# Columns outside the related square: summed as adjacency bytes times bf16 parts, scaled at the end

## The reference, cut to what matters

```
h = max(layernorm(x), 0)
q, k = per head (8 heads of 64): h[sub] @ Wq.T + bq,  h[obj] @ Wk.T + bk      # 10000 related pairs, indices < 1500
scores[head, sub, obj] = q . k / 8;  0 on the other neighbours;  -inf where adj is 0;  1e-7 on the diagonal
attn = softmax(scores, axis=2)
x = x + (attn.sum over heads / 8) @ h
```

## Time and profile before

| | us |
|---|---|
| median of 3 runs | 1131.22 |
| lowest, highest run | 1126.92, 1132.14 |
| the profiled execution | 1126.64 |
| its span, first to last instruction | 1124.9 |
| TensorE busy, whole span | 1050.8 |
| VectorE busy, whole span | 917.9 |
| ScalarE busy, whole span | 786.5 |

### The profile page before, as it was taken

One profiled execution on the slowest core, in us unless ns is written; L12 is line 12 of the kernel. 1 busy time (PEld: TensorE's weight loads), 2 busy tenths in 40 slices (PEclk: granted clock), 3 DMA queues, 4 the chain that ended last, 5 costly groups with the idle time before them and its releaser, 6 DMA issues. The chain is left out here.

```text
span 1124.9 us, 25112 instructions
## 1 busy us (share of the span) xinstructions
PE 1050.8 (93%) x10560; PEld 715.8 (64%) x10565; DVE 917.9 (82%) x1259; ACT 786.5 (70%) x833; POOL 277.0 (25%) x272
## 2 busy tenths in 40 slices
PE   1999997999999999999988599999999999999997
PEld 1444443444444444444444499999999999999743
DVE  2355146899999999999981899999999999999466
ACT  1244336777777777776633799999999999998122
POOL 2778750000000000000000244334344344434000
PEclk9999998999999999999999799999999999999999
DMA  9640443322212221100054587767777777777311
GB/s 336 162 29 2 114 91 77 79 68 68 66 40 41 68 59 59 38 20 29 23 215 155 156 196 186 183 171 180 183 187 183 191 203 180 181 182 184 122 69 75
DMA packets 71552, 136.45 MB, mean 121 GB/s; under 512 B 9237, under 2 KB 18834, under 8 KB 69394
## 3 DMA queue, kind: packets, MB, share of 16 engines
q1 hardware_dynamic: 50386, 101.19, 25.7%
q0 software_dynamic: 21056, 33.67, 20.4%
HBM read 92.92 MB, written 25.04 MB: 105 GB/s over the span
## 5 line engine op out<-in xcount | busy, mean ns | idle before, releaser
L1511 ACT ACTIVATE area_h<-area_a,keep 128x2048 fp8e4<-128x2048 f32 x197 | 376.8, 1989 | 4.2 <-PE psum L1666 4.1
L1665 PE MATMUL psum<-s_V,area_h 128*128 128x99 bf16 x3072 | 298.1, 209 | 0.8 <-DVE area_b L1437 0.5
L1665 PEld LDWEIGHTS psum<-s_V,area_h 128*128 128x128 fp8e4 x3072 | 283.4, 98 | 1.1 <-DVE area_h L1561 0.7
L1666 PE MATMUL psum<-s_V,area_b 128*128 128x99 bf16 x2048 | 204.1, 209 | 0.0
L1666 PEld LDWEIGHTS psum<-s_V,area_b 128*128 128x128 fp8e4 x2048 | 189.5, 97 | 0.0
L743 PE MATMUL psum<-area_h,f_region 128*128 128x512 f32 x384 | 184.9, 596 | 0.0
L1185 DVE SCALAR_TENSOR_TENSOR f_region<-area_b,s_r,f_region 128x1500 f32<-128x1500 f32 x96 | 170.8, 1779 | 2.2
L1561 DVE TENSOR_TENSOR area_h<-area_h,area_a 128x512 uint32<-128x512 uint32 x256 | 167.9, 686 | 4.4
L1196 DVE CUSTOM_DVE_ANT_0 area_b<-psum,late 128x1500 f32<-128x1500 f32 x96 | 161.1, 1715 | 8.2 <-PE psum L658 8.1
L1668 PE MATMUL psum<-s_V,area_h 128*128 128x198 bf16 x1024 | 150.0, 249 | 13.7 <-DVE area_h L1561 13.7
L977 ACT ACTIVATE area_b<-area_b,s_negm 128x1500 f32<-128x1500 f32 x96 | 147.8, 1540 | 20.9 <-DVE s_negm L1196 19.9
(11 more groups left out here) (185 smaller groups left out, 1423.0 us busy)
## 6 DMA issues: line engine op xcount, KB each, us to landing
area_a<-s_rows SPq DMA_DIRECT2D x16, 1024.0 KB, 7.2
late<-area_h POOLq DMA_DIRECT2D x64, 256.0 KB, 4.4
late<-far_rows SPq DMA_DIRECT2D x60, 256.0 KB, 4.1
area_b<-area_h POOLq DMA_DIRECT2D x48, 256.0 KB, 4.6
area_b<-far_rows SPq DMA_DIRECT2D x45, 256.0 KB, 3.5
rel_planes<-f_h SPq DMA_DIRECT2D x3, 2304.0 KB, 15.9
late<-rel_planes SPq DMA_DIRECT2D x36, 192.0 KB, 2.6
area_h<-in_x SPq DMA_DIRECT2D x4, 1024.0 KB, 12.9
```

Source lines behind the costliest of these rows:

```text
L1511: act.activation(masks[:, j, :], s1b[:, b, :], ACT.Relu, bias=t["s2"][:, n, 0, j:j + 1], scale=BIG, saturate=False).then_inc(signs, 1)
L1665: pe.matmul(out[:, :, 0:DZ], masks[:, j, cols], V[:, b, j, :, 0:DZ], **first)
L1666: last = pe.matmul(out[:, :, DZ:CZ], fars[FAR.index(j)][:, cols], V[:, b, j, :, DZ:CZ], **then)
```

## The change

The weight rows `W` keep only the 1536 columns that can carry scores (AG = 6 pairs instead of HA = 8). The other four column blocks are summed apart, per row block, as in `gather`: the adjacency chunk, fp8 bytes that hold NEAR = 2, is loaded back from `adj_chunks`, and twelve bf16 matmuls (four blocks, three parts) sum it against h. VectorE multiplies the sum by `half`, which is c / 2, and adds it to x (`finish_far`). The far sum of block r uses bank 7 (bank 1 and 2 for the last two blocks), and the aggregate of block r starts in the same bank when `based` says that the far sum has been read. The bf16 parts are kept from the front on (`keep_parts`), in places freed for them: the marked relations now overwrite plane 0 in place, and `sq` has one buffer instead of two. `finish` adds only the near sum. Head additions are all on VectorE, as they were.

```diff
+AG = ET // 2
...
-        self.W = [region[:, i * N:(i + 1) * N] for i in range(2)]
+        self.W = [region[:, i * N:i * N + NE] for i in range(2)]
...
-        self.sq = [region[:, at + D * i:at + D * (i + 1)] for i in range(2)]
+        self.sq = region[:, at:at + D]
...
+            def load_far(i):
+
+                k = NU - 1 + i
+                sp.wait_ge(chunk_out[place(k)], 16 * (stored(k) + 1))
+                if i:
+                    sp.wait_ge(far_in, 16 * i)
+                if i >= 2:
+                    sp.wait_ge(far_summed, i - 1)
+                else:
+                    sp.wait_ge(f.proj, GROUPS)
+                sp.dma_start(f.far_chunk[i % 2], t["adj_chunks"][tile_at(k)][:, ET * P:].rearrange("p (j i) -> p j i", j=4)
+                             ).then_inc(far_in, 16)
 
             def load_related(r):
                 if r >= 2:
-                    sp.wait_ge(f.marked, r - 1)
+                    sp.wait_ge(f.low_ready, r - 1)
+                    sp.wait_ge(f.nbr_ready, r - 1)
...
                 if n + NU + 3 < NT:
                     store_chunk(n + NU + 3)
+                if n + 2 <= ET:
+                    load_far(n + 2)
...
+            def sum_far(i, bank, alone):
+
+                pe.wait_ge(far_in, 16 * (i + 1))
+                if i == 0:
+                    pe.wait_ge(f.parted, 2 * NT + 5)
+                for b in range(NT - ET):
+                    moving = (f.upper(h[:, ET + b, :]), f.far_rest[b // 2][:, b % 2, :], f.far_tail[b])
+                    for part in range(3):
+                        first, final = b == 0 and part == 0, b == NT - ET - 1 and part == 2
+                        last = pe.matmul(ps[:, bank, :], f.far_chunk[i % 2][:, b, :], moving[part],
+                                         start=alone and first, stop=alone and final)
+                last.then_inc(far_summed, 1)
+
+            def unrelated(r):
+
+                if r == 0:
+                    pe.wait_ge(based, NU)
+                elif r < ET - 2:
+                    pe.wait_ge(summed, NU + r)
+                else:
+                    pe.wait_ge(masked, HA * ET)
+                sum_far(r + 1, far_bank(r), True)
...
             def aggregate(r, m, blocks=(0, 1)):
 
-                order = tuple(range(HA)) if r < ET - 1 else (6, 7, 0, 1, 2, 3, 4, 5)
-                if m == order[0] and r < ET - 1:
-                    pe.wait_ge(*((summed, NU + r) if r else (based, NU)))
+                if m == 0 and blocks[0] == 0 and r < ET - 2:
+                    pe.wait_ge(based, NU + r + 1)
+                if m == 0 and blocks[0] == 0 and r == ET - 2:
+                    pe.wait_ge(summed, NU + r)
...
                 if scored:
                     score(n + 1, 0)
+                if turned:
+                    unrelated(r)
                 project(n + 1)
                 add_blocks(n, 0, (0,))
...
                 add_blocks(n, 4, (1,))
-                if turned:
-                    turn_w(r, 6)
-                add_blocks(n, 5)
                 if chunked:
                     turn_adj(ka, 3)
                 if scored:
                     score(n + 1, 3)
-                if turned:
-                    turn_w(r, 7)
-                add_blocks(n, 6)
+                add_blocks(n, 5, (0,))
                 turn_h(n + 2)
-                add_blocks(n, 7)
+                add_blocks(n, 5, (1,))
...
-                act.activation(W[r % 2][:, :], adjn[:, (r + NU) % ADJ_RING, :], ACT.Copy, scale=cd[:, 0:1]).then_inc(w_started, 1)
+                act.activation(half[:, r % 2:r % 2 + 1], cd[:, 0:1], ACT.Copy, scale=1.0 / NEAR).then_inc(w_started, 1)
+                act.activation(W[r % 2][:, :], adjn[:, (r + NU) % ADJ_RING, 0:NE], ACT.Copy, scale=cd[:, 0:1]).then_inc(w_started, 1)
...
+            def keep_parts():
+
+                dve.wait_ge(f.proj, GROUPS)
+                dve.wait_ge(f.parted, 2 * NT)
+                for i in range(2):
+                    upper = f.rest[:, ET + 2 * i:ET + 2 * i + 2, :].bitcast(BF16).rearrange("p t (c w) -> p t c w", w=2)[:, :, :, 1]
+                    dve.tensor_copy(f.far_rest[i], upper).then_inc(f.parted, 1)
+                dve.tensor_copy(f.far_tails, f.tail[:, ET:ET + 2, :]).then_inc(f.parted, 1)
+                for b in (2, 3):
+                    dve.tensor_copy(f.far_tail[b], f.tail[:, ET + b, :]).then_inc(f.parted, 1)
...
+            def finish_far(r):
+                k = r + NU
+                dve.wait_ge(far_summed, r + 2)
+                dve.wait_ge(w_started, 2 * (r + 1))
+                dve.wait_ge(x_in[k % 3], 16 * (k // 3 + 1))
+                dve.scalar_tensor_tensor(xt[k % 3][:, :], ps[:, far_bank(r), :], half[:, r % 2:r % 2 + 1], xt[k % 3][:, :],
+                                         ALU.mult, ALU.add).then_inc(based, 1)
+
             def finish(r):
                 k = r + NU
-                dve.wait_ge(agg, NU + HA * (r + 1))
-                dve.wait_ge(x_in[k % 3], 16 * (k // 3 + 1))
+                dve.wait_ge(agg, NU + AG * (r + 1))
+                dve.wait_ge(based, NU + r + 1)
...
                 for p in range(PAIRS):
                     for hd in (2 * p, 2 * p + 1):
                         add_head(n, hd)
+                    if p == 0 and n:
+                        finish_far(n - 1)
                     for hd in (2 * p, 2 * p + 1):
                         if n + 1 < ET:
                             mask(n + 1, hd)
             front()
             for n in range(ET):
                 step(n)
+            finish_far(ET - 1)
```

More of the change, by code:

```diff
@@ L95, in __init__ @@
         self.low = [late[:, (2 * PLANES + 2 * i) * words:(2 * PLANES + 2 * i + 2) * words].bitcast(BF16) for i in range(2)]
-        self.scored = late[:, (2 * PLANES + 4) * words:(2 * PLANES + 5) * words].bitcast(F8)
+        last = (2 * PLANES + 4) * words
         self.wnat = [late[:, i * KT * D:(i + 1) * KT * D].rearrange("p (k d) -> p k d", k=KT) for i in range(2)]
@@ L112, in __init__ @@
         at += KT * D
-        self.sq = [region[:, at + D * i:at + D * (i + 1)] for i in range(2)]
+        self.sq = region[:, at:at + D]
+        at += D
+        self.far_rest = [region[:, i * N + NE:(i + 1) * N].bitcast(BF16).rearrange("p (t d) -> p t d", t=2) for i in range(2)]
+        self.far_tails = region[:, at:at + D].bitcast(BF16).rearrange("p (t d) -> p t d", t=2)
+        self.far_tail = [self.far_tails[:, 0, :], self.far_tails[:, 1, :],
+                         late[:, last:last + D // 2].bitcast(BF16), sb("far_tail", [P, D], BF16)[:, :]]
+        far_chunk = [late[:, last + D // 2:last + D // 2 + P].bitcast(F8), sb("far_chunk", [P, 4 * P], F8)[:, :]]
+        self.far_chunk = [c.rearrange("p (j i) -> p j i", j=4) for c in far_chunk]
         self.h2 = sb("h2", [P, D])
@@ L180, in mark_related @@
         dve.wait_ge(self.cleared, r + 1)
[L181 to L184, removed]
+        scored = self.scored(r).bitcast(U32)
+        dve.tensor_tensor(scored, scored, near, ALU.bitwise_and).then_inc(self.marked, 1)
         dve.wait_ge(self.marked, r + 1)
[L186 removed]
+        dve.tensor_tensor(near, near, scored, ALU.bitwise_xor).then_inc(self.nbr_ready, 1)
     def first_low(self, dve):
         dve.wait_ge(self.marked, 1)
[L190 removed]
+        dve.tensor_scalar(self.low[0][:, 0:NREL], self.scored(0)[:, 0:NREL], BIG, -BIG, ALU.mult, ALU.add).then_inc(self.low_ready, 1)
     def make_low(self, act, it):
@@ L493, in stage2 @@
     cd = sb("cd", [P, 2])
+    half = sb("half", [P, 2])
     stats = sb("stats", [P, 6])
@@ L500, in stage2 @@
     chunk_out = [sem(f"chunk_out{i}") for i in range(3)]
-    seq_out = [sem(f"seq_out{i}") for i in range(2)]
+    seq_out = sem("seq_out")
     wseq_in, a_in = sem("wseq_in"), sem("a_in")
@@ L515, in stage2 @@
     DIRECT = NT - 3
+    LINKS = 6
     no = bank_rounds()
-    heads.place(chunk, sq[0])
+    heads.place(chunk, sq)
     def place(k):
@@ L624, in load_adj @@
                 else:
-                    pool.wait_ge(w_started, last - NU + 1)
+                    pool.wait_ge(w_started, 2 * (last - NU + 1))
                 f.load_adj(pool, io, k)
@@ L706, in gather_f32 @@
                     j = 2 * m + b
-                    last = pe.matmul(ps[:, 7, :], W[1][:, j * P:(j + 1) * P], h[:, j, :], start=(j == 0), stop=(j == NT - 1))
-                if m == HA - 1:
+                    if j == ET - 1:
+                        sum_far(0, 7, False)
+                    last = pe.matmul(ps[:, 7, :], W[1][:, j * P:(j + 1) * P], h[:, j, :], start=(j == 0), stop=(j == ET - 1))
+                if j == ET - 1:
                     last.then_inc(agg, 1)
+            def sum_far(i, bank, alone):
[17 more added lines that the diff above has]
+                sum_far(r + 1, far_bank(r), True)
             def turn(r, m):
@@ L743, in aggregate @@
                     last = pe.matmul(ps[:, 7 if r < ET - 1 else 0, :], WT[m % 2][:, b, :], h[:, 2 * m + b, :],
```

(6 more changed lines are left out.)

118 lines of the change are left out of this document (57 added, 61 removed).

## The result

The changed kernel takes 1149.16 us (median of 4 runs, 1148.19 to 1149.94) against 1129.17 us (median of 4 runs, 1126.92 to 1132.14) for the kernel before on the same chip: 1.7% slower, ratio 1.0171 [1.014, 1.0202]. The forecast was 1148 us. The profiled execution took 1148.58 us, its span 1146.8, against 1126.64 and 1124.9.

A forecast was written before the change was run, and what follows sets the result against it. VectorE was taken to set the step period, TensorE close behind. Step 0 -0.3, steps 1 to 10 +17.7, tail -4.5, clock +7.5: +20.4 on 1126.64 gives 1147.0, plus 1 for a low profiled run: 1148; range 1128 to 1160.

The forecast's parts named there:

- VectorE waits 1.39 us for the second score pair: Steps 1 to 10: late scores hold VectorE ahead of head 2's mask; step 1.88 us longer, 17.7 us in all.
- The chain: Within a step: `finish_far` frees bank 7 at 10.16 us after the previous step's head 7 mask; second pair starts at 15.37.
- The wait of 0.19 us forecast at the third pair: Within a step: third score pair readable at 25.16 us, VectorE ready for it at 24.97.
- TensorE's own way: Turn, scores, far sum and projection before bank 7: TensorE ready 9.90 us after the previous step's head 7 mask.
- The 0.27 us ahead of the diagonal: VectorE's wait in each step for the scaled copy: goes, gain 0.27 us.
- the 0.77 us: VectorE's wait in each step for the last exponential: stays.
- The clock: Gaps of 2.5 us at step ends lower TensorE's clock in five of ten steps, 1.5 us each: +7.5 us.
- The tail: Last row blocks: two pairs of column blocks fewer for each, two far sums more, some new waits: -4.5 us.
- The sum: Whole kernel: step 0, steps 1 to 10, tail and clock together, +20.4 us.
- Rival 3: Steps and tail: VectorE never waits for TensorE, the 0.77 us wait goes; -8.6 us, 1118 us; chance 0.10.

The follow-up runs named there:

- e6: Changed kernel with `finish_far` behind the first head addition instead of the second, full far sum kept: 1143.65 us, ratio 1.0107.
- e2: Changed kernel with 11 of the 12 matmuls of every far sum left out: 1160.92 us, ratio 1.023.
- e3: Changed kernel with 11 of 12 far-sum matmuls left out and `finish_far` behind the first head addition instead of the second: 1130.95 us, ratio 1.0002.
- e4: Changed kernel with seven matmuls, result never read, put in TensorE's gap at the end of steps 1 to 10: 1145.57 us, ratio 1.012.
- e7: The kernel before, unchanged, profiled once more: 1130.71 us, span 1129.0.
- e8: From e5, with the normalized block's transposition ahead of the fourth score pair and the next weight rows' first turn behind it: 1120.44 us, ratio 0.9902.
- e5: Changed kernel with the far sum in TensorE's end-of-step gap (bank 0), `finish_far` ahead of the factors, first score pair behind the projection: 1135.76 us, ratio 1.0036.
- e1: Changed kernel with near sums 1 and 3 moved behind score pairs 1 and 2, all work kept: 1146.77 us, ratio 1.0138.
- e10: The kernel of e8 run once more, beside the kernel before on one chip: 1122.2 us, ratio 0.9908.

## Why the prediction was right

*Where the loss comes from.* Predicted: steps 1 to 10 lengthen since VectorE waits 1.39 us for the second score pair. Measured: 1.28 us, step +1.79 instead of +1.88, and 34.81 - 33.34 = 1.47 instead of 1.33 for the last two. The chain stood as forecast: `finish_far` 746 ns, bank 7 at T0 + 10.08 (forecast 10.16), second pair at T0 + 15.27 (15.37). The wait of 0.19 us forecast at the third pair shows only as a mask that starts 0.08 us behind the end of the addition before it instead of overlapping it.

*What sets it.* The prediction put it on bank 7 and counted TensorE's own way as ready 0.26 us earlier, T0 + 9.90 against 10.16. The trace has 0.20 us of idle time, and e6 has TensorE there at 9.71, 0.37 before the 10.08. So the second lock stood in the prediction, and its weight was underrated: e6 shows that opening the bank gives back 0.4 of 1.8, e2 that shortening TensorE's way gives back nothing, e3 that both together give back all but 0.1.

*The gains.* The 0.27 us ahead of the diagonal went, the 0.77 us stayed, L1018 takes 1.56 us as interpolated, and `half` makes nobody wait in these steps. `keep_parts`, the chunk loads and the single `sq` cost nothing in the steps; none of them is in a wait of the step.

*The clock.* Forecast: it falls behind five of ten gaps of 2.5 us, at 1.5 us each. Measured: five of ten gaps of 2.16 us; 36.49 - 35.21 = 1.28 us each in four steps, and one in the tail. e4 shows that the gap is the cause. That the count was met exactly is luck: it was set between one gap behind which it fell and one behind which it held, and the second of these does not repeat (below).

*The tail.* Forecast -4.5 us, measured -2.5, with the fifth fall of the clock in it, in the far sum of block 10, and one copy late:

```profile
589.15 0.44 PE L770 MATMUL psum<-ident,f_region 128*128 128x128 f32 x2 [2.16 <-ACT f_h2T L1006]
589.42 0.39 PE L754 MATMUL psum<-area_h,f_far_chunk 128*128 128x512 bf16 x1
...
593.71 3.60 PE L820 MATMUL psum<-f_region,f_h2T 128*128 128x512 f32 x8
...
617.52 1.08 PE L788 MATMUL psum<-s_w,f_h2T 128*128 128x32 f32 x8 [0.69 <-ACT area_b L992]
```

That far sum took 593.71 - 589.42 = 4.29 us instead of 2.64. The 1.65 between them belong to the clock; without them the tail is 4.15 us shorter, 0.35 off the forecast, and the late copy of 0.69, where 0.2 was allowed for new waits, is more than that. The tail of the kernel before is not one number either: in its second profile (e7) the clock fell there and it took 558.7, and beside that one the change saves 4.2.

*The sum.* Forecast -0.3 + 17.7 - 4.5 + 7.5 = 20.4. Measured: step 0 +0.04; eight steps at 1.79 and two at 1.47, +17.3; the tail -4.15; the clock 4 x 1.28 + 1.65 = +6.8; and the front +2.0, which the forecast left out and which is no more than the two profiles of before differ by: 21.9 from unrounded terms. Without the front it is 19.9 against the 20.4.

*Rival 3,* faster at 1118 us if bank 7 were free early and the 0.77 us wait went too, comes near what e8 made, 1120.4, but not by its own sum. It priced -0.37 a step and -4.5 in the tail; beside the first profile of before, e8's eleven steps are 5.0 us shorter together, its tail 6.4, and its front ends 6.1 later. Nor was its condition enough: in e6 the bank was free at T0 + 8.20, earlier than the 8.8 that it asked for, and VectorE waited on, because TensorE's own way, the 9.90 of the forecast, was left out of the condition. The places of the far sum, of `finish_far` and of two copies decide together on which side the change falls.

## What to carry to other kernels

When work is moved, price the place before the amount: 1.0 us of TensorE work saved per step cost 1.8, since what came instead stood ahead of the one result that another engine was waiting for. Look for a second lock close behind the one that the profile names: behind a wait of only 0.20 us at the bank stood TensorE's own way, so that opening the bank gave back 0.4 and not 1.8. An idle stretch of one engine is a place for new work, if what fills it needs no copy that stands behind long instructions in a third engine's queue.

## What the runs showed of the hardware

The clock behind equal gaps. In the changed kernel it fell behind five of ten gaps of 2.16 us, in e6 behind three of ten of the same length, in e3 behind nine of ten. Gaps of 1.22 us (e5, ten of them) and of 1.61 us (e1, eight of them) left it at 1.00; behind e1's one gap of 2.16 us it fell. The gap of 1.65 us that left it at 1.00 in the first profile of before did not in the second: in e7 it is followed by

```profile
569.37 4.97 PE L764 MATMUL psum<-f_region,f_h2T 128*128 128x512 f32 x7 [1.65 <-ACT f_region L923]
```
```profile
570.00:573.40 3.40, 3.40 (x6) 1.34 (x5) 2.00 (x9) 2.00 (x1) 0.76 (x15) 0.50 1.05 408
```

a granted clock of 0.50, and the projection took 4.97 us, against 3.70 in the first. One observation of a gap without a fall is no proof that the next will have none.

The front of one and the same kernel ended at 200.5 and at 202.85 us, and those of the kernels with this change between 201.8 and 209.7. In the two profiles of the kernel before it went with the end of GpSimd's scatters: VectorE's joining of the planes behind them started at 166.41 and at 170.25 us. What makes the scatters end later was not tried. They are not the whole spread: from that joining to the first scaled copy it is 32.6 to 35.5 us in most profiles, and 36.8 in those of e5, e8 and e10. What costs these three more was not followed.
